# Routing stage: the late softmax's end and attention blocks 2 and 3 placed behind group 0's normalization, and a block's weights of four batches written by one operation

## The reference, cut to what matters

```python
x = x + conv(group_norm(x))                 # a memory that is learnt over 32 steps
t = to_tokens(x)
# attention in a band of 32 keys around each query
a = softmax(e - 10000 * (1 - band)); t = t + a @ layernorm(t)
# feed-forward with 8 experts, top 2
logits = layernorm(t) @ Wr + br
top_p, top_idx = top_k(softmax(logits), 2); weights = top_p / top_p.sum()
y = gelu(xe @ W1 + b1) @ W2 + b2            # xe: normalized tokens, per expert
t = t + (weights * y[top_idx]).sum()
```

## Time and profile before

| what | value |
|---|---|
| median of 3 runs | 971.86 us |
| the profiled execution's own time | 972.06 us |
| its span, first to last instruction | 970.2 us |
| mean granted TensorE clock in it | 0.940 |
| busy: PE, DVE, ACT, POOL | 84%, 74%, 64%, 63% |
| the stage: first VectorE operation of `experts` to the end of the last scatter's issue | 696.0 to 808.5 us of the span |

### The profile page before, as it was taken

The page is one execution under the profiler, slowest core; times in us unless marked ns, Lnnn a source line. Parts: engine busy times, 40 slices in busy tenths (PEclk is TensorE's granted clock), DMA queues, the critical chain, the costliest instruction groups (busy, mean ns, idle before and its releaser), DMA issues. The chain is left out here.

```text
span 970.2 us, 25223 instructions
## 1 busy us (share of the span) xinstructions
PE 811.6 (84%) x8069; PEld 506.3 (52%) x8069; DVE 722.1 (74%) x1846; ACT 618.1 (64%) x1384; POOL 608.7 (63%) x758
## 2 busy tenths in 40 slices
PE   2888999999999999999999989847677746999950
PEld 2455555555555555555555544411355524999940
DVE  4586888888888888888888853669788651777747
ACT  4577777777878777787777832248534503888830
POOL 1127887878878788787888839810007772666650
PEclk8899999999999999999999999967999867999985
DMA  7007999994000000000000033032001111333327
GB/s 235 1 2 148 157 207 158 65 6 2 0 0 0 0 0 0 0 0 0 0 0 0 0 90 87 0 104 90 3 4 54 49 53 53 83 90 92 93 67 237
DMA packets 105406, 54.10 MB, mean 56 GB/s; under 512 B 42624, under 2 KB 96664, under 8 KB 105360
## 3 DMA queue, kind: packets, MB, share of 16 engines
q1 hardware_dynamic: 98976, 43.34, 28.9%
q0 software_dynamic: 4544, 9.38, 3.0%
q10 hardware_dynamic: 1840, 0.79, 0.4%
HBM read 21.49 MB, written 29.44 MB: 52 GB/s over the span
## 5 line engine op out<-in xcount | busy, mean ns | idle before, releaser
L398 POOL TENSOR_TENSOR s_w<-s_xsh,s_w_mem 128x512 f32<-128x512 f32 x186 | 251.8, 1354 | 8.9 <-DVE s_w_mem L570 3.4
L570 DVE SCALAR_TENSOR_TENSOR s_w_mem<-s_w_mem,s_eta,lp_g 128x256 f32<-128x256 f32 x496 | 217.8, 475 | 24.0 <-PE lp_g L733 18.6
L495 ACT ACTIVATE s_xsh<-s_w,l_keep_lr 128x256 f32<-128x256 f32 x384 | 173.8, 505 | 17.5 <-POOL l_keep_lr L418 17.4
L1484 POOL DMA_INDIRECT f_yg<-f_yr,f_xmeta x78 | 78.4, 1005 | 54.5 <-DVE f_yr L1823 41.7
L1479 POOL DMA_INDIRECT f_xg<-f_xrow,f_place x64 | 64.0, 999 | 48.0 <-DVE f_place L1719 28.8
L403 POOL TENSOR_TENSOR s_xsh<-s_w,l_keep 128x512 f32<-128x512 f32 x64 | 72.1, 1126 | 0.0
L1459 ACT ACTIVATE f_hh<-fp_v,f_bcol 128x256 f32<-128x256 f32 x156 | 61.1, 476 | 13.1 <-DVE f_hs_lo L1814 5.6
L489 ACT COPY l_wt<-lp_b 128x512 f32<-128x512 f32 x96 | 56.4, 588 | 15.0 <-PE lp_b L719 15.0
L719 PE MATMUL lp_b<-s_cst,s_w 128*128 128x128 f32 x384 | 61.7, 284 | 0.0
L1588 PE MATMUL fp_v<-f_xf,s_w_hi 128*128 128x256 bf16 x312 | 55.3, 279 | 1.6 <-DVE f_xmeta L1803 1.2
L707 PE MATMUL lp_h<-s_w,l_gf 128*32 128x128 f32 x1024 | 41.2, 278 | 18.3 <-ACT l_gf L482 18.3
(11 more groups left out here) (345 smaller groups left out, 2036.1 us busy)
## 6 DMA issues: line engine op xcount, KB each, us to landing
f_xg<-s_pad SPq DMA_DIRECT2D x1, 17280.0 KB, 107.5
f_xt<-f_xg SPq DMA_DIRECT2D x39, 130.0 KB
r_w<-in_L_ffn_W_dram SPq DMA_DIRECT2D x16, 256.0 KB, 3.1
s_w<-f_yg SPq DMA_DIRECT2D x16, 256.0 KB, 3.9
xs<-in_x_dram SPq DMA_DIRECT2D x4, 512.0 KB, 6.8
t_w<-in_L_ffn_W_dram SPq DMA_DIRECT2D x8, 256.0 KB
out_dram<-s_x SPq DMA_DIRECT2D x8, 256.0 KB, 3.2
s_xsh<-s_xl SPq DMA_DIRECT2D x4, 448.0 KB, 3.5
```

What stands on the lines that cost most here:

```text
L398: nc.gpsimd.tensor_tensor(W[k][:, half(h), :], KW[k][:, half(h), :], M[k][:, half(h), :], ALU.add).then_inc(w_ready[k], 1)
L495: m = nc.scalar.mul(KW[k][:, b, :], W[k][:, b, :], keep_lr[:, b:b + 1])
L570: i = nc.vector.scalar_tensor_tensor(out=M[k][:, b, :], in0=M[k][:, b, :], scalar=eta[:, b:b + 1], in1=ps_g[b][:, 0:256], op0=ALU.mult, op ...
L1484: nc.gpsimd.indirect_dma_start(sb["yg"][:, :], bass.IndirectOffsetOnAxis(ap=xmeta[:, j, a, 0:1].bitcast(mybir.dt.int32), axis=0), yr[j % R ...
```

## The change

Four things are done.

1. In `masked(n)` one operation of 128x512, with both inputs broadcast, takes the place of four of 128x128. This holds for all 8 blocks.
2. On VectorE `valued(0)` moves ahead of the late softmax's sum. `valued(1)`, `spread(0)` and `normed(0)` move ahead of the late softmax's reciprocal and product. `remainder(0)` follows the product, then `masked(2)`.
3. `routed(0)` gets `masked(3)` as work to do where it waits for the exponential. `valued(2)`, `masked(4)` and `valued(3)` follow `routed(0)`; before, `valued(2)` stood ahead of it.
4. TensorE and ScalarE take blocks 2 and 3 in the matching places: `weights(2)`, `values(2)` behind `router(0)`, and `weights(3)`, `values(3)` behind `counts(0)`; `turned_weights(2)` behind `features(0)`, and `turned_weights(3)` behind `odds(0)`.

Groups 1 to 3 keep their order. The 16 unused matmuls at the head of group 1 keep their place in the loop, which now is behind `values(3)`.

```diff
@@ scalar
                 for g in range(GR):
-                    if 2 * g + 2 < NTB:
+                    if g >= 1 and 2 * g + 2 < NTB:
                         turned_weights(2 * g + 2)
                     roots(g)
                     rows(g)
                     features(g)
-                    if 2 * g + 3 < NTB:
+                    if g == 0:
+                        turned_weights(2)
+                    elif 2 * g + 3 < NTB:
                         turned_weights(2 * g + 3)
                     second(g)
                     odds(g)
+                    if g == 0:
+                        turned_weights(3)
@@ tensor
                 for g in range(GR):
                     if g >= 1:
                         unused(nc, sb, ps_am, 16)
-                    if 2 * g + 2 < NTB:
+                    if g >= 1 and 2 * g + 2 < NTB:
                         weights(2 * g + 2)
                         values(2 * g + 2)
                     router(g)
-                    if 2 * g + 3 < NTB:
+                    if g == 0:
+                        weights(2)
+                        values(2)
+                    elif 2 * g + 3 < NTB:
                         weights(2 * g + 3)
                         values(2 * g + 3)
                     counts(g)
+                    if g == 0:
+                        weights(3)
+                        values(3)
@@ vector
                 def masked(n):
                     if n >= 2:
                         dve.wait_ge(at_done, n - 1)
-                    for b in range(B):
-                        nc.vector.tensor_tensor(am[n % 2][:, b, :].rearrange("p (r j) -> p r j", j=WIN),
-                                                e[:, n, b:b + 1, :].to_broadcast([128, 4, WIN]), band, ALU.mult)
+                    nc.vector.tensor_tensor(am[n % 2][:, :, :].rearrange("p b (r j) -> p b r j", j=WIN),
+                                            e[:, n, :, :].rearrange("p b (a j) -> p b a j", a=1).to_broadcast([128, B, 4, WIN]),
+                                            band.rearrange("p (a r) j -> p a r j", a=1).to_broadcast([128, B, 4, WIN]), ALU.mult)
...
-                def routed(g):
+                def routed(g, meanwhile=lambda: None):
...
                     nc.vector.tensor_tensor(both[:, :, :].rearrange("p e n -> p n e"), one[:, :, :], two[:, :, :], ALU.add).then_inc(count_ready, 1)
+                    meanwhile()
                     dve.wait_ge(ex_ready, g + 1)
...
                 nc.vector.tensor_tensor(er, er, bc, ALU.subtract).then_inc(soft, 1)
+                valued(0)
                 dve.wait_ge(sb["exp_ready"], 2)
                 nc.vector.tensor_reduce(m_late, er, AX.X, ALU.add).then_inc(soft, 1)
-                valued(0)
+                valued(1)
+                spread(0)
+                normed(0)
                 dve.wait_ge(soft, 10)
                 nc.vector.reciprocal(m_late, m_late).then_inc(soft, 1)
                 dve.wait_ge(soft, 11)
                 nc.vector.tensor_tensor(er, er, bc, ALU.mult).then_inc(soft, 1)
+                remainder(0)
                 dve.wait_ge(soft, 12)
                 masked(2)
-                valued(1)
-                for g in range(GR):
+                routed(0, lambda: masked(3))
+                valued(2)
+                masked(4)
+                valued(3)
+                for g in range(1, GR):
```

## The result

The changed kernel took 977.84 us, the median of 19 executions (972.91 to 980.52). The kernel before took 973.01 us in 19 executions beside it (970.40 to 980.49). The ratio is 1.0039, with a 95% interval of 1.0020 to 1.0057: the change makes the kernel slower by 3.8 us, between 1.9 and 5.5 (the ratio compares executions taken side by side; the two medians lie 4.8 us apart). One later execution of the changed kernel, in the repeat e7, took 1172.46 us at a mean granted clock of 0.64 and is left out of its ratio. The prediction was wrong. It forecast no change, at 972.0 with a range of 970.6 to 973.9. The profiled execution of the changed kernel took 977.60 us.

A forecast was written before the change was run, and what follows sets the result against it. GpSimd's scatters, full from first to last, were taken as the bound, dated by groups 0 and 1's `place`. 972.06 - 0.71 (group 1) + 0.72 (clock) = 972.07, less 0.2 about 971.9, leaned to 972.0; range 970.6 to 973.9.

The forecast's parts named there:

- Group 0, 3.18 us sooner at full clock: VectorE's reciprocals for group 0 start at 706.66 instead of 709.84, and its `place` is 3.18 us sooner.
- The root is 0.61 behind its arguments, the mask takes 0.61, `masked(3)` fits into the wait for the exponential: In group 0: reciprocals 0.61 us behind the root's arguments, 128x512 mask 0.61, `masked(3)` (0.8) within VectorE's 0.99 us wait.
- The new wait of `values(3)` and the 16 behind it: In group 1, TensorE waits for `valued(2)`, then runs values and 16 unused matmuls; VectorE idles about 1.9 us, reciprocals 0.42 later.
- GpSimd's wake-up: From group 1's `place` to the 17th scatter: 0.96 us, as for the first scatter; with 0.3 the gain would be 1.4.
- one fall: Main case: TensorE's clock falls only ahead of group 0's transposes; 971.9 us, chance 0.42.
- The first idle time lets the clock fall, for 0.72 us: TensorE, idle 3.9 us ahead of group 0's transposes, drops to the low clock; reciprocals to logits cost 0.72 us more.
- the sign of a wrong sum for group 0: Stated check in the changed kernel's profile: the first scatter is not over 2 us sooner.
- The second fall: Rival: clock falls in 2.9 us idle ahead of `values(3)`, slowing values and 16 matmuls by 1.9, up to 3.8 us.
- two falls: Rival: clock falls ahead of group 0's transposes and again ahead of `values(3)`; 972.8 to 975 us, chance 0.34.
- the rival's +1.9 for the 17th scatter: In group 1, half of 3.8 us, if the clock is back midway through the 16 matmuls; result 973.8, two falls' chance 0.34.
- The range: Whole kernel: 970.6 to 973.9 us, from no fall with quick wake-up to the middle of two falls.
- The rule of the Trainium skill: On TensorE, idle gaps between matmul bursts let the clock drop; sum 0.0 with it, -0.7 without.

The follow-up runs named there:

- e7: The changed kernel again, nothing altered, beside the kernel before; 977.84 us, ratio 1.0023 (1.0000 to 1.0047).
- e8: The changed kernel with four 128x128 mask operations per block again, leaving only its new order; one execution, 981.37 us.
- e3: The changed kernel with 16 more unused matmuls ahead of values(3)'s wait, the old 16 kept behind it; 975.15 us, ratio 1.0023 against the kernel before.
- e6: The changed kernel with 20 more unused matmuls ahead of group 0's transposes, filling only the first idle time; one execution, 977.78 us.
- e9: As e5, with more unused matmuls in the idle times of groups 1 to 3 too; 968.94 us, ratio 0.9949 against the kernel before.
- e5: As e1, with 20 more unused matmuls ahead of group 0's transposes, so both idle times are filled; 969.19 us, ratio 0.9942 against the kernel before.
- e10: The same kernel as e5, measured once more beside e9; 971.60 us, ratio 0.9957 against the kernel before.
- e1: The changed kernel with group 1's 16 unused matmuls moved ahead of values(3)'s wait for valued(2); 972.90 us, ratio 0.9995 against the kernel before.
- e4: The kernel before with the single mask operation alone, no order changed; 973.21 us, ratio 0.9997 against the kernel before.
- e2: The changed kernel with group 1's 16 unused matmuls left out; 973.52 us, ratio 1.0011 against the kernel before.
- b1: The kernel before, unchanged, run again for a second trace of its stage; one execution, 970.91 us.

## Why the prediction was wrong

Point by point:

- *Group 0, 3.18 us sooner at full clock.* Right: reciprocals at 710.04 - 699.65 = 10.39 against 13.65, 3.26 sooner, in every trace with the new order but e8's. With the first idle time filled the first scatter was at 25.9 in three traces of four, 3.25 sooner.
- *The root is 0.61 behind its arguments, the mask takes 0.61, `masked(3)` fits into the wait for the exponential.* Right: 0.45 us in place of 0.61, a mask of 0.69 that overlaps the next by 0.09, and 0.24 us of waiting left.
- *The new wait of `values(3)` and the 16 behind it.* Right in place and size at full clock: 4.1 us in e3, where VectorE stood idle ahead of group 1's reciprocals for 1.95 us (1.9 predicted).
- *GpSimd's wake-up.* Wrong for the 17th scatter: I took the 0.96 us of the first one for it too. In the changed kernel group 1's `place` is ready at 751.41 + 0.17 = 751.58 and the 17th starts at 751.86, 0.28 later; it is 0.27 to 0.28 in e3 and e7. So with one fall the 17th should have come 0.68 us sooner than in my sum. In e3, which has the first fall alone, it came 0.94 sooner than that sum (49.03 in place of 49.97) and 0.93 sooner than in the kernel before, where the sum had no change.
- *The first idle time lets the clock fall, for 0.72 us.* That it falls was right (3.76 us idle, 3.9 predicted). The size was taken from the one row at hand, group 3's, where the clock came back in time for the router. When it doesn't, the price is 1.9 to 2.2 us, as in four of six traces; in e7 the first scatter was then only 0.5 us sooner than before, which the prediction gave as the sign of a wrong sum for group 0.
- *The second fall.* This is the step that failed: between an idle time of 2.09 that left the clock alone and 4.89 that didn't, I put 2.9 on the side of the shorter one and gave one fall 0.42 and two falls 0.34. Both traces of the changed kernel have the second fall, behind idle times of 3.17 and 2.74 us, and so has e6. Its price was 2.8 us in the first trace and 1.5 in e7 (from the values to block 4's transposes 6.92 and 5.60 in place of 4.10), where I took 1.9. In the first trace the 16 cost 1.6 us more, the half that I had put in; the values cost 1.2 more (2.72 to the first of the 16 in place of 1.49), where the sum had 0.3. That the rival's +1.9 for the 17th scatter was nearly met (+2.25 in the one trace, +2.5 in the other) is in part luck: the price was too low, and the wake-up that I had added was 0.68 too high. The two rows at hand, 2.09 and 4.89, couldn't decide an idle time of 2.9.
- *The range.* Of the 5.8 us between forecast and result 1.2 are the kernel before's own, whose median was 973.01 beside the changed kernel and 971.86 when I predicted. Of the rest, 3.8 us by the ratio, the stage explains 2.6: the mean of 114.05 and 113.08 against 110.95. What is left is not in it. The stage's start lay at 696.2 to 697.5 us in six of the fourteen traces, at 698.3 in e9, and at 699.5 to 701.3 in the other seven, although none of the kernels changes code ahead of it. e5 and e10 are one kernel, and their starts are 696.93 and 700.56. So executions of one kernel differ there by some 3.5 us. In the trace of the changed kernel TensorE was idle for 2.84 us at 620 us and the clock was low behind it; its matmuls there, L1021, took 3.14 us in place of 1.88:

```profile
623.12 1.12 PE L1048 MATMUL rp_t<-s_cst,s_xl 128*128 128x128 f32 x4 [2.84 <-DVE s_xl L1076]
624.02 3.14 PE L1021 MATMUL rp_a<-r_h,s_first 128*128 128x512 f32 x4
```

The same place in e3, which starts the stage early:

```profile
622.55 0.66 PE L1048 MATMUL rp_t<-s_cst,s_xl 128*128 128x128 f32 x4 [2.84 <-DVE s_xl L1076]
623.04 1.88 PE L1021 MATMUL rp_a<-r_h,s_first 128*128 128x512 f32 x4
```

The low clock at this place is in all seven traces with a late start and in none of the other seven.

The three executions known before (970.84 to 972.05) lay within 1.2 us, and I took their spread for the kernel's. 19 executions span 10 us, and a range of 3.3 us was too narrow for a median of either kernel. Whether the change brings the late start more often than chance is open: both traces of the changed kernel have it, and five of the nine others with some part of the change (e1, e4, e6, e8, e10), but none of the three of the kernel before. Those three are of executions of 970.88 to 972.06 us. Of the kernel before's 100 executions in all series 39 took over 976 us, and no trace shows one of these; of the changed kernel's 30 (without the one of 1172.46) it is 25. So the 2.6 us is the stage's loss against the lower part of the kernel before's times. It lies within the interval of the ratio, but that it is the whole of the 3.8 isn't shown.

The rule of the Trainium skill that the prediction weighed, page "TensorE: Matmul & The Clock Gate", section "HAM oscillation — how this bites in real kernels", was borne out, and more strongly than I used it: in both traces of the changed kernel both gaps between bursts had a low clock behind them (idle times of 3.8 us, and of 3.2 and 2.7), and where a gap was filled, the burst right behind it ran at full clock.

## What to carry to other kernels

When work is taken out of a path to start a saturated engine sooner, ask at once what feeds its second portion: in e6 group 0 moved by 3.2 us, and the 17th scatter still came 1.5 us later than before. Put matmuls that only keep TensorE busy ahead of a wait and not behind it, where they lie in the path of what was waited for; the same 16 cost the change its gain in the one place, and in the other gave, with the first idle time filled too, a kernel 0.4% to 0.6% faster than the one before. And look for each new idle time of TensorE that a reordering opens: the clock can be at half behind it, and what runs there may lie in a path.

## What the runs showed of the hardware

- The length of an idle time of TensorE alone doesn't decide whether the clock is low behind it. At 620 to 625 us, ahead of L1048, the same idle time of 2.83 to 2.84 us stands in twelve of the fourteen traces: in seven the transposes behind it took 1.11 or 1.12 us (half clock), in five 0.65 or 0.66 (full). Ahead of `values(3)` the clock was low behind 3.2 us (changed kernel, e6) and 2.7 us (e7). Behind 2.5 us (e2, e8) the values ran at full clock, 1.13 us, but what followed them at half: block 4's transposes 1.11 us in e2, the 16 some 4.3 us in e8. In b1 the transposes behind an idle time of 2.08 us took 0.66 us, and those behind 1.93 and 2.04 us took 1.11 and 1.12.
- The router's 16 matmuls with 8 columns take 1.90 us at full and 3.42 us at half clock. In e1, e7 and e8 the clock was low through all 16 of group 0; in the changed kernel and e3 it rose in time, and they took 1.93 and 1.94.
- A 128x512 product on VectorE with both inputs broadcast takes 0.69 us, like a plain one; four of 128x128 and this one differ by 0.2 us.
- GpSimd's 16 scatters of a group took 20.8 to 21.9 us from the first to the 17th in the traces where the 17th waited for nothing (20.8 in the kernel before, 21.9 in e4), single ones up to 1.86 us in place of 0.96 (changed kernel). The first scatter starts some 0.96 us behind its `place`, the 17th, where it waits, 0.28.
